# A macaron block on one NeuronCore: a periodic table of due times replaced by a written order of every engine

## The reference

```python
x = x + 0.5 * ffn_fp4(layernorm(x))        # "front"
x = x + mamba(layernorm(x))                # "head", then "scan"
x = x + 0.5 * ffn_fp4(layernorm(x))        # "back"
x = x + 0.5 * lora_moe(layernorm(x))       # "lora" (first)
x = x + attention(layernorm(x))            # "attention"
x = x + 0.5 * lora_moe(layernorm(x))       # "lora" (second)
```

## Time and profile before

| | us |
|---|---|
| median of 3 runs | 4890.47 |
| lowest, highest run | 4883.07, 4906.68 |
| span of the profiled execution | 4905.3 |
| PE, DVE busy in the span | 4033.8, 3994.1 |
| ACT, POOL busy in the span | 2371.7, 1600.0 |

### The profile page before, as it was taken

The page is one execution under the profiler, slowest core; times in us unless marked ns, Lnnn a source line. Parts: engine busy times, 40 slices in busy tenths (PEclk is TensorE's granted clock), DMA queues, the critical chain, the costliest instruction groups (busy, mean ns, idle before and its releaser), DMA issues.

```text
span 4905.3 us, 54168 instructions
## 1 busy us (share of the span) xinstructions
PE 4033.8 (82%) x18222; PEld 2046.2 (42%) x18251; DVE 3994.1 (81%) x5964; ACT 2371.7 (48%) x4341; POOL 1600.0 (33%) x1036
## 2 busy tenths in 40 slices
PE   4556678888989898888989898988989898786867
PEld 2223334443535354444435354444435353434343
DVE  6578889898989989898989889898989899684402
ACT  2334344555555464645555554646555554543322
POOL 0143433333334333333333333333333343332000
PEclk8778889999999999999999999999999999897867
DMA  1477668767676777777677777787677777772100
GB/s 56 118 176 180 149 170 182 174 158 185 159 171 175 163 177 175 180 166 178 158 177 178 157 176 159 177 179 180 156 176 173 159 176 161 181 174 64 42 23 28
DMA packets 241433, 753.39 MB, mean 154 GB/s; under 512 B 37650, under 2 KB 132659, under 8 KB 171524
## 3 DMA queue, kind: packets, MB, share of 16 engines
q1 hardware_dynamic: 241156, 749.95, 64.9%
HBM read 647.30 MB, written 101.71 MB: 153 GB/s over the span
## 4 chain that ended last, share of the span: by engine, by line
PE 47%; DVE 23%; ACT 11%; DMA 9%; issue 4%; SPq 3%; POOL 2%; ACTq 0%; DVEq 0%; POOLq 0%
PE m L1135 8%; DVE state L1608 5%; PE m L1107 5%; DVE mt L1696 4%; DMA decay<-dt_scratch 4%; DMA state<-dtx_scratch 3%; PE y L1212 2%; PE pd L1334 2%; PE m L1149 2%; DVE u L1603 2%; PE y L1201 2%; DMA dt_scratch<-front 2%; ACT shared L982 2%; PE m L1136 1%; ACT decay L912 1%
## 5 line engine op out<-in xcount | busy, mean ns | idle before, releaser
L731 POOL TENSOR_TENSOR state<-state,bc 128x1024 f32<-128x1024 f32 x512 | 1215.7, 2375 | 1764.9 <-DVE u L1603 1764.8
L1608 DVE TENSOR_TENSOR_SCAN state<-decay,u 128x1024 f32<-128x1024 f32 x512 | 1168.6, 2282 | 13.0 <-ACT decay L912 1.0
L912 ACT ACTIVATE decay<-decay,a_neg 128x511 f32<-128x511 f32 x1024 | 671.3, 712 | 268.8 <-DMA decay<-dt_scratch 268.5
L1107 PE MATMUL m<-w_gu,hats_m 128*128 128x480 f32 (+1 forms) x1536 | 699.3, 588 | 39.0 <-DVE front L1523 31.6
L1603 DVE TENSOR_TENSOR u<-state,bc 128x1024 f32<-128x1024 f32 x512 | 632.5, 1235 | 81.1 <-DMA state<-dtx_scratch 70.7
L1135 PE MATMUL m<-w_dn,front 128*128 128x256 f32 (+1 forms) x1536 | 447.7, 440 | 46.3 <-ACT front L849 46.2
L715 POOL TENSOR_TENSOR front<-front,hsc_m 128x704 f32<-128x704 f32 x128 | 205.8, 1608 | 809.8 <-DVE front L1433 809.8
L1107 PEld LDWEIGHTS m<-w_gu,hats_m 128*128 128x128 f32 x1536 | 287.7, 198 | 295.1 <-issue 215.8
L1135 PEld LDWEIGHTS m<-w_dn,front 128*128 128x128 f32 (+1 forms) x1536 | 308.1, 214 | 181.3 <-ACT front L849 89.9
L1201 PE MATMUL y<-state,sel 128*32 128x512 f32 x2048 | 288.8, 638 | 92.5 <-POOL state L731 91.3
L1149 PE MATMUL m<-hats_m,w_in 128*128 128x512 f32 x512 | 270.5, 662 | 69.1 <-DVE front L1562 38.4
(11 more groups left out here) (264 smaller groups left out, 7177.6 us busy)
## 6 DMA issues: line engine op xcount, KB each, us to landing
decay<-dt_scratch SPq DMA_DIRECT2D x256, 1024.0 KB, 7.3
state<-dtx_scratch SPq DMA_DIRECT2D x256, 1024.0 KB, 11.5
qk_scratch<-shared SPq DMA_DIRECT2D x64, 384.0 KB, 3.1
shared<-qk_scratch SPq DMA_DIRECT2D x384, 64.0 KB
kh<-qk_scratch SPq DMA_DIRECT2D x384, 64.0 KB
xs_scratch<-front SPq DMA_DIRECT2D x16, 1024.0 KB, 5.7
dt_scratch<-front SPq DMA_DIRECT2D x256, 64.0 KB, 2.9
dtx_scratch<-hats_m SPq DMA_DIRECT2D x256, 64.0 KB, 1.9
```

What stands on the lines that cost most here:

```text
L731: eng.tensor_tensor(st, st, bc[:, 1:2, :].to_broadcast([P, WIDE, L]), ALU.mult).then_inc(scan_pool.sem, scan_pool.step(f"c{r}{h}"))
L912: ins = eng.activation(d, d, ACT.Exp, scale=a_neg[:, g:g + 1])
L1107: mm = eng.matmul(f.bank(f"gu{t}{p}")[:, 0:2 * width], norm.hat_t[:, k, t * P:(t + 1) * P], w_gu[:, k, 2 * lo:2 * (lo + width)], start=(k ...
L1608: eng.tensor_tensor_scan(st, decay[:, n % ND, h * WIDE * L:(h + 1) * WIDE * L], u[:, :], 0.0, ALU.mult, ALU.add).then_inc(scan_dve.sem, sc ...
```

## The change

`ORDER` takes the place of the tables: for each engine a string with one digit (the thread, 0 to 3) for every step of the whole program, 5792 for DVE, 4992 for PE, 4208 for ACT, 2415 for SP and 1024 for POOL. `weave` follows it. The threads themselves run through all samples in the same sequence of parts as before. Most instructions (or pairs) now have a `yield` of their own. `KEEP` is empty, so `keep` issues nothing. On SP the store of `dtx` waits for `dtx{c}` and no longer for `zero{c}`. Some waits stand in another step than before: `dtx_stored` directly in front of the first normalised copy, the wait for `qk_saved` in front of the first of the twelve head loads. No other instruction is added, removed or resized.

```diff
+ORDER = {
+    "DVE":
+        "33333333333333330000000000000000000000000000000000000000000000000000333333333333333333330003000030000300003000000000000000000000"
...
+def weave(order, *threads):
+
+    for t in threads:
+        next(t, None)
+    for n in order:
+        next(threads[int(n)], None)
+    assert all(next(t, "end") == "end" for t in threads)
...
-        KEEP = {"a": 1, "e202": 2, "e311": 1, "e330": 4, "in4": 19, "in6": 8, "last2": 1, "m0": 1, "m2": 2, "rest3": 1, "sum8": 12}
-        PERIOD = 261.4610
-        PE_PLAN = (
...
+        KEEP = {}
...
+        def run(order, lead, ffn, head, scan, lora, attention):
+
+            def first():
+                for w, n in WORK:
+                    yield from head(n) if w == "head" else ffn(w == "front", FFNS.index((w, n)), n)
...
+            def third():
+                for i in range(B):
+                    yield from lora(i, 2 * i, 3 * i)
+                    yield from attention(i, 3 * i + 1)
+                    yield from lora(i, 2 * i + 1, 3 * i + 2)
+
+            weave(order, first(), second(), third(), ahead())
...
                 for c in range(C):
-                    yield 40 + 2.8 * c
-                    eng.wait_ge(head_dve.sem, head_dve.after(i, f"zero{c}"))
-                    for src, dst, done in ((dt, dt_scratch, dt_saved), (dtx_of(i), dtx_scratch, dtx_saved)):
+                    for name, src, dst, done in (("zero", dt, dt_scratch, dt_saved), ("dtx", dtx_of(i), dtx_scratch, dtx_saved)):
                         for j in range(Q):
+                            yield
+                            if j == 0:
+                                eng.wait_ge(head_dve.sem, head_dve.after(i, f"{name}{c}"))
                             eng.dma_start(dst[i, c].rearrange("(q e j) l -> j (q e) l", q=Q, j=Q)[j], src[32 * j:32 * (j + 1), c % 2, :]
                                           ).then_inc(done[c % 2], 16)
...
                 eng.tensor_reduce(mx, blocks(src), AX.X, ALU.max, apply_absolute_value=True).then_inc(*mark("max"))
+                yield
                 wait("max")
                 eng.tensor_scalar(scale, mx, -1.0 / 6.0, -1e-12, ALU.mult, ALU.min).then_inc(*mark("scale"))
+                yield
                 eng.tensor_scalar(nudged, mx, NUDGE / 6.0, 1e-12, ALU.mult, ALU.max).then_inc(*mark("nudged"))
...
-                    yield 37.5 + 2.8 * c
+                    yield
                     eng.wait_ge(head_act.sem, head_act.after(i, f"one{c}"))
                     eng.scalar_tensor_tensor(out=one[:, b, :], in0=one[:, b, :], scalar=-1.0, in1=dt[:, b, :],
                                              op0=ALU.add, op1=ALU.subtract).then_inc(head_dve.sem, head_dve.step(f"rest{c}"))
+                    yield
                     eng.wait_ge(head_dve.sem, head_dve.after(i, f"rest{c}"))
                     eng.wait_ge(head_act.sem, head_act.after(i, f"ln{c}"))
                     eng.tensor_tensor(lnx[:, b, :], lnx[:, b, :], one[:, b, :], ALU.subtract).then_inc(head_dve.sem, head_dve.step(f"log{c}"))
```

## The result

The median of four runs is 4859.48 us, against 4891.32 for the kernel before on the same chip: a ratio of 0.9927, 95% interval 0.9903 to 0.9951. So the change is worth 0.7%, where 4.3% had been forecast. The profiled execution took 4869.6 us with a span of 4867.8.

A forecast was written before the change was run, and what follows sets the result against it. VectorE was taken as the nearest limit; 69.2 + (891.4 - 40) + 3144 + 253.9 + (418.0 - 45) = 4691.5 us against 4905.3, on the median 4680. Range 4530 to 4910, the forecast's own 4570 to 4800.

The forecast's parts named there:

- the written order, steady part: Twelve steady samples: removed VectorE stalls, with the neighbour gain, bring a sample from 272.7 to 262.0 us, -129 in all.
- Neighbours: VectorE, steady part: about 40 fewer dependent neighbouring instructions a sample at 0.13 us each, -5.3 us a sample.
- Stalls: VectorE, steady part: logarithm wait -3.6, half of L1682's 2.4, all others 0.6 together; sum -5.4 us a sample.
- threads can change at every operation: VectorE: another thread's instruction can stand between any two, so fewer dependent neighbours, -5.3 us a sample.
- The earlier third thread: End of program: third thread starts sample 14 58 us of VectorE work before the last scan's end, delaying that scan; unpriced.
- Zero products: TensorE, steady part: removing 52 products, 13.8 us a sample, counts as zero because waiting hides them.
- the rival's point of 0.905: Slower-clock rival, steady part: below TensorE clock 0.905 samples exceed 272.7 us; at 0.87, 282.4 and 5005 in all; chance 0.06.
- Moved waits and transfers: SyncE's row transfers and stores, and other moved waits: 0 taken, +11.5 us a sample kept for the range.
- Filling: Program start to the third scan's end, 891.4 us: a quarter of VectorE's idle time goes, -40, bounds 0 and -80.
- Emptying: Last scan's end to program end, 418.0 us: third thread begins its last sample earlier, -45, bounds 0 and -71.
- Order too rigid: Rival, all engines: order laid out for wrong durations makes threads wait; VectorE stalls double (21.7 more), 5085 us; chance 0.05.
- Given back: Rival: one decay or state load a sample issued late costs 11.5 us; time stays about 4890; chance 0.07.

The follow-up runs named there:

- run 5: Kernel before's order and zero products; on VectorE another thread's step put between dependent neighbours, 23 places a sample: ratio 1.0335 to the kernel before.
- run 17: New kernel with GpSimd's product by C cut to 1 of 512 positions: ratio 0.98 to the kernel before.
- run 4: Old order up to 4100 us, then the new one, with the old zero products: 4842 us, ratio 0.9889 to the kernel before.
- run 2: Kernel before with an empty table of zero products, all else as it was: 4934 us, ratio 1.007 to the kernel before.
- run 1: New kernel with the old zero products put back at the same sites: 4907 us, ratio 1.0021 to the kernel before.
- run 3: New code with the old order and old zero products, so only moved waits and smaller steps differ: ratio 1.0012 to the kernel before.
- run 6: New kernel with the scan's state sums four steps later on TensorE (three or fewer for 13 of 256): ratio 1.0503 to the kernel before.
- run 7: New kernel with the back half's norm later on VectorE, behind 12 us of other work: ratio 1.0007 to the kernel before.
- run 13: New kernel with only the 52 sums in front of which TensorE waited one step later: ratio 0.9969 to the kernel before.
- run 14: New kernel with 254 of the 256 scan's sums one step later on TensorE: ratio 1.0198 to the kernel before.
- run 15: New kernel with 45 held VectorE instructions moved behind one to three steps that GpSimd cannot hold: ratio 0.9971 to the kernel before.
- run 9: New order with ten middle samples made alike by averaging each step's place, no zero products: ratio 1.1039 to the kernel before.
- run 10: Order half-way between old and new by mean virtual times, no zero products: ratio 1.2062 to the kernel before.
- run 11: New order with the scan's sums one or two steps earlier on TensorE, no zero products: ratio 1.061 to the kernel before.
- run 16: New order to 820 us, old to 4100, then new, old zero products, with 9 held VectorE places moved: ratio 0.9831 to the kernel before.

## Why the prediction was wrong

**The step that failed is "the written order, steady part"**: 262.0 forecast, 281.2 measured. The median, 4859, lies outside the forecast's own range of 4570 to 4800, and two of its signs failed with the step: VectorE was idle 35.2 us a sample instead of under 20 ((3374.9 - 2952.80) / 12), and the clock was under 0.93. The step's pieces:

- *Neighbours* (-5.3 a sample): right in size. Overlaps and gaps gave (39.9 + 19.2) / 12 = 4.9. But the swaps of run 5 did not collect it, and here it came with other things that ate it.
- *Stalls* (-5.4): wrong, +8.6 (103.1 / 12). I had measured how much work the new order puts behind each logarithm, and that wait did shrink, by 1.5 a sample rather than 3.6. The wait of L1682, of which half was to go, grew by 1.4. I then took "all other stalls" as a small gain bounded by zero. They could grow, and did: the text said that what replaces a removed stall is the next late producer, and the bound did not follow from it.
- *Holding by GpSimd*: no term at all, +4.7 (56.8 / 12) in VectorE's records; run 17 returned 33 us of the 102, 2.7 a sample. VectorE's rows of before could not price it (nothing held in twelve samples), but the trace did show GpSimd's product released by VectorE's `u` nearly every time (1764.8 of its 1764.9 us of idle time) and GpSimd's own instructions held beside `u` (L715, above). The question "what runs beside it, and can it?" was open. The Trainium skill, page "SBUF — State Buffer", section "SBUF: two separate sides", has the rule: VectorE and GpSimd share one pair of ports by an exclusive lock, and a VectorE instruction with two SBUF inputs or in a two-port mode is blocked for the whole GpSimd instruction if that starts first. The runs agree (L1624, 2.85 against 0.69), but for the scan, which has two SBUF inputs and was not held in 157 cases. It was the rule that spoke against "threads can change at every operation", and I weighed another.
- *The earlier third thread*: I noted that its work "now delays the last scan instead", and gave it no price. In run 4 the sample in which it is moved up took 25 us more, 2.1 a sample over twelve. That the new order pays the same, and for this reason, is not shown.
- *Zero products* (0): not far off. Their loss costs 1.5 a sample in the old order (run 2), and putting them back into the new one costs 3.0 (run 1). TensorE's clock fell to 0.91 in the steady part, near the rival's point of 0.905, and TensorE was busy 239.5 a sample (2873.80 / 12) where 227.0 was forecast; 227.0 x 0.96 / 0.91 is 239.5, so the rival's stretching of the work took place. It does not by itself give 281.2, since with the rival's 31.9 of idle time a sample would take 271.4; TensorE's idle time rose to 41.7. The missing products are not what lowered the clock in this order: run 1 has them and the same 0.91. How much of VectorE's stalls comes from TensorE's slower work, and whether the waits lowered the clock or the clock lengthened the waits, no run separates.
- *Moved waits and transfers* (0): right (run 3).

What stays open is the division of the stalls' 103 us. Runs 6, 7, 13, 14 and 15 each took one wait or hold away, or most of it, and none gained on the new kernel; so the surplus cannot be ascribed to one wait. 33 of the 102 us go with GpSimd's product (run 17). Some 25 may belong to the third thread or the seam, taken over from run 4. The rest, some 44 us or 3.7 a sample, is open: the fit of single steps, of which runs 5, 6, 9, 10, 11 and 14 show only that an order is sensitive to it, and the lower clock.

**Filling** (-40, bounds 0 and -80): -27.1. The first scan and the second, as in the earlier trace rows, gave 9.5 and 10.9:

```profile
69.20:421.30 352.10, 214.46 (x580) 94.10 (x579) 240.27 (x317) 128.67 (x219) 97.81 (x56) 0.74 0.59 144
421.30:660.10 238.80, 164.04 (x530) 84.32 (x531) 208.87 (x266) 102.55 (x179) 102.74 (x60) 0.78 0.71 165
```

**Emptying** (-45, bounds 0 and -71): -109.9, beyond the bound. The mechanism, that the third thread starts its last sample earlier, was right. The two rows (timeline of ScalarE) are the last residual of the last back half and the end of sample 14 in the third thread, as in the earlier trace rows:

```profile
4679.80 0.38 ACT L887 ACTIVATE xx<-m 128x256 f32<-128x256 f32 x1 [2.61 <-PE m L1180]
...
4688.11 0.60 ACT L971 ACTIVATE xx<-pu 128x512 f32<-128x512 f32 x1 [2.86 <-PE pu L1298]
```

The third thread is 8.5 us behind the back half (4688.7 - 4680.2), where "within 30" was asked; before it was 70.9. But the back half itself ended 120.5 us after the last scan (4680.2 - 4559.7), before 162.7. I had taken that as fixed, and it is the term that was mis-sized: 42 us. The likely reason is that less of the third thread's work is left beside it (after the last scan VectorE runs 266 instructions instead of 286, ScalarE 196 instead of 227); no run tests it.

**The rivals.** "Order too rigid" came nearest: it put the stalls at +21.7 a sample and had 0.05. What happened is less than half of it (+8.6), together with gains at the ends that the rival ignored. "Given back" came near in size (4890, measured 4859) for the wrong reason: VectorE's wait for state loads did not grow (27.0 us before, 16.4 after), and the loss is in other stalls and in holding. That the total came out a little below that of before is luck in so far as a loss of 102 us in the steady part and gains of 140 at the ends happened to cancel nearly. The two slow rivals and the forecast were treated as exclusive; the result is a sum of parts of each.

## What to carry to other kernels

A step that a schedule puts next to another is priced by what else it touches, not only by its dependences: before weaving threads finely on VectorE, look in the trace for instructions of either engine that take longer than their kind beside the other (here those with two SBUF inputs, and small TENSOR_SCALAR and CAST), and lay the first order out so that they do not meet. In a finished order, moving them apart won nothing (runs 15 and 16). When an order of in-order queues is replaced, judge each stage by itself and combine the winners by hard cuts; that gave 1.9% where the new order gave 0.7%. Stalls that remain in a tuned order are not a stock of gain: here, of five runs that removed one from the new order, none was faster.

## What the runs showed of the hardware

- A VectorE instruction with two SBUF inputs begun 0.07 us after a GpSimd product took 2.85 us for 0.69 and ended 0.55 after it. Single-input ones of 0.19 us (L1480, 128 x 44) were held too, for 0.6 to 2.1 us. Instructions that read PSUM, the norms' statistics, the reductions (31 of L1477 with over 0.3 us of a product to run) and the scan (157) were not.
- The other direction exists: in the kernel before, 30 products that began 0.17 us after L1550 (two SBUF inputs, 0.68 us) took some 2.74 us instead of 2.35, and 31 of 128 rescalings (L715), begun while `u` ran, took 2.30 instead of 1.39. By this count (over 0.3 us above the shortest of their kind) GpSimd was held for 65 us before and 81 after.
- In the summary of a group this is invisible in the median (L1629 and its like L1560, 691 ns in both kernels) and shows only in the maximum and mean (2658 and 802 ns, before 693 and 692).
